# Attention scores seeded with their negated row maxima by ScalarE and VectorE, in place of a fourth matmul product

## The chip, the cores and the metric

The kernel runs on one core of a Trainium2 chip. The metric is the device time of one execution in microseconds; lower is better. The engines are TensorE (PE in the profile), VectorE (DVE), ScalarE (ACT), GpSimd (POOL) and the sync engine (SP), which only issues transfers.

## The reference

A self-attention block on x of shape (4, 512, 48, 48), that is 4 batches of 512 channels by T = 2304 tokens. With 32 groups of channels and 8 heads of 64 channels:

```python
xn = group_norm(x) * gn_w + gn_b
q, k, v = split(qkv_w @ xn + qkv_b)              # per head, 64 channels each
weight = softmax(q.T @ k / 8, axis=-1)           # 2304 x 2304 per head, fp32
a = v @ weight.T
out = xn + proj_w @ a + proj_b
```

The softmax takes each query's maximum over all keys off its scores before the exponential. Scores are made from a high and a low part of q and k (fp32r values), so that three products give nearly fp32 precision.

## The kernel before

The work runs as 4 batches, each of 4 head pairs. A pair's queries are cut into CH = 6 blocks of N = 384, and its keys into KT = 18 tiles of 128. A *step* is one key tile against one query block for both heads of the pair; a block has 18 steps, a batch 432. Two steps make a *slot* (GS = 2), so a block has 9 slots, numbered 0 to 8 here. Every engine has its own program with its instructions in a fixed order, and semaphores join them. In slot i, with steps 2i and 2i+1, the engines do the following.

- **TensorE**: one *max unit* (`max_unit`, L498: 128 queries against 384 keys, high parts only, for both heads, into `aux_banks`), then `make_scores` for step 2i and step 2i+1 (L532, four products each: k_hi q_hi, k_lo q_hi, k_hi q_lo, and one_rows max_row, each for two heads), then a second max unit, then a part of the projections (*prep*) of a later q, k or v chunk into `pool_bank` (L476, L488), then `make_pv` for the steps of the slot before (L550). In slot 2 of a block, `finish` (L519) sums the denominators. The max units run AHEAD = 24 steps ahead of the scores, since a query's maximum must be known before its scores are finished.
- **ScalarE**: `exponentials` for both steps (L743, from the scores bank to one of 8 `probs` buffers), then what a finished prep needs (`high_part` L692 or `v_group` L696), and once per block the copies of `oacc` (L728) and of the sums (L708).
- **VectorE**: for each max unit a reduction over 384 keys (`unit_max`, L842), which frees `aux_banks` for the next unit, since there is only one such buffer; in slots 3, 4 and 5 of a block one piece of a reciprocal per step (`take_recip`, L917), the last followed by the product `o_norm` (L923, both inputs in SBUF); the low part of a finished q or k chunk (`low_part`, L835); and at step 11 of a block, in slot 5, `negate_max` (L848), which reduces the 6 partial maxima of 3 x 128 queries and both heads. Pair 3 of the first three batches also has the statistics of the next batch (L864) and its coefficients (L882 to L908).
- **GpSimd**: adds each step's probabilities into `denom` (L1057), 17 additions of 128x768 per block. An exponential waits for the addition of 8 steps before.
- **SP**: weights, x, the results and `put_max_row` (L350).

The negated maxima lie in columns, one query per partition, and the scores need them in a row. `max_rows` (L504) turns them over with one TensorE product against `ident`, ScalarE copies them (L703), and two small transfers put them into `max_row`. The fourth product then adds that row to each score.

The last pair of the last batch has no max units. After the four pairs of a batch comes its output projection (L631), and at the start of a batch ScalarE waits until the previous batch's output is stored. In the pairs 0 to 2, three preps are spread over each block in quarters by `SPREAD`; pair 3 runs them whole in written slots.

Of the kernel before, what the change touches and what calls it, by code (L numbers as in the profile page):

```python
# [5 lines left out]
def attention_block_program(nc, x, gn_w, gn_b, wqkv_t, bqk, bv, wproj_t, bproj, att, out):  # L6
# [47 lines left out]
    SPREAD = (((0, 0, 2), (1, 2, 4)), ((3, 0, 1), (4, 1, 3), (5, 3, 4)), ((7, 0, 2), (8, 2, 4)))  # L54
# [10 lines left out]

    def maxrow_slot(j):
        last_unit = QT * CH * (j + 1) - 1
        return (last_unit - AHEAD) // GS + 1

    def batch_plan(more_batches):  # L70
# [7 lines left out]
        for p in range(PAIRS):  # L78
# [17 lines left out]
            for j in range(1, CH):  # L96
                whole(before, s0 + maxrow_slot(j), ("maxrow", p, j))
            if p < PAIRS - 1 or more_batches:
                whole(before, s0 + SLOTS + maxrow_slot(0), ("maxrow", p + 1, 0))
# [26 lines left out]
    def first_order():  # L126
# [7 lines left out]
        order.append(("maxrow", 0, 0))  # L134
# [26 lines left out]

    with ExitStack() as ctx:
# [10 lines left out]
        max_row = sb("max_row", [128, T], fp32r)  # L173
        one_rows = sb("one_rows", [128, 128], fp32r)
# [15 lines left out]
        ident = sb("ident", [128, 128])  # L190
# [3 lines left out]
        neg_max = sb("neg_max", [128, D])  # L194
        row_parts = sb("row_parts", [2 * QT, 128], fp32r)
# [70 lines left out]
        aux_done = sem("aux_done")  # L266
        neg_ready = sem("neg_ready")
        max_row_in = sem("max_row_in")
# [61 lines left out]
        def _(sp):  # L330
# [15 lines left out]
            def put_max_row(j, u):  # L346
                wait_free(sp, u)
                for e in range(2):
                    dst = max_row[e * D:e * D + 1, chunk(j)].bitcast(fp32).rearrange("o (t q) -> o t q", q=128)
                    sp.dma_start(dst, row_parts[e * QT:(e + 1) * QT, :].bitcast(fp32)).then_inc(max_row_in, 16)  # L350
# [7 lines left out]
            def stream(b, last):  # L358
                before, _ = PLANS[last]
                nb = b + 1  # L360
                for s in range(BSTEPS):
# [10 lines left out]
                    if s in NORM_STEPS and not last and NORM_STEPS[s] + XPARTS < XITEMS:  # L372
                        n = NORM_STEPS[s]
                        sp.wait_ge(xn_ready, XITEMS * (b + 1) + n + 1)
                        load_x(nb, XITEMS + n + XPARTS)
                    if s in PUT_AT:
                        put_block(b, PUT_AT[s])
                    if s % GS < GS - 1:
                        continue
                    for key in completed(before[s // GS]):  # L380
                        if key[0] == "maxrow":
                            put_max_row(key[2], use(b, last, key))
                        elif key == ("q", p, CH - 1) and not (last and p == PAIRS - 1):
# [55 lines left out]
            put_max_row(0, FIRST_USES["maxrow", 0, 0])  # L439
# [13 lines left out]
            sp.wait_ge(max_row_in, 32 * BLOCKS * B)  # L453
# [5 lines left out]
        def _(pe):  # L459
# [63 lines left out]
            def score_part(s, b, product):  # L523
                p, j, kt = s // STEPS, s % STEPS // KT, s % KT
                if product == 0 and s >= 2:
                    pe.wait_ge(probs_ready, PROBS_PRIMED + BSTEPS * b + s - 1)
                elif product == 3 and kt == 0:
                    pe.wait_ge(max_row_in, 32 * (BLOCKS * b + p * CH + j + 1))
                ks, qs = ((k_hi[p % 2], q_hi), (k_lo[p % 2], q_hi), (k_hi[p % 2], q_lo), (one_rows, max_row))[product]
                kcols = slice(kt * 128, (kt + 1) * 128) if product < 3 else slice(0, 128)  # L530
                for e in range(2):
                    last = mm(scores[:, s % 2, e, 0:N], ks[head(e), kcols], qs[head(e), chunk(j)],  # L532
                              start=(product == 0), stop=(product == 3))
                if product == 3:
                    last.then_inc(scores_full, 1)

            def make_scores(s, b):
                for product in range(4):
                    score_part(s, b, product)
# [26 lines left out]
            def behind(key, since, until, b, last):  # L566
# [18 lines left out]
                elif kind == "maxrow":  # L585
                    max_rows(CH * pairs + i + 1, u)
# [51 lines left out]
            pe.wait_ge(consts_made, 8)  # L638
            units = 0
            for key in FIRST:  # L640
# [23 lines left out]
                elif kind == "maxrow":  # L664
                    max_rows(1, u)
# [7 lines left out]
            for k in range(FIRST_BANKS):  # L673
                pe.wait_ge(bank_free[k], first_count(k))

# [10 lines left out]
        def _(act):  # L686
# [11 lines left out]

            def max_rows(u, rows_sent):
                wait_full(act, u)  # L700
                if rows_sent is not None:
                    act.wait_ge(max_row_in, rows_sent)
                a(row_parts[:, :], bank(u)[0:2 * QT, 0:128], ACT.Copy).then_inc(bank_free[u[0]], 1)  # L703
# [41 lines left out]

            def behind(key, b, last):
# [8 lines left out]
                elif kind == "maxrow":  # L755
                    max_rows(u, 32 * (CH * (PAIRS * b + p) + i))
# [5 lines left out]
            def stream(b, last):  # L762
                before, after = PLANS[last]
                for i in range(PAIRS * SLOTS):
# [31 lines left out]
            for s in (o_saved, proj_saved):  # L796
# [322 lines left out]
```

## Time and profile before

| | before |
|---|---|
| median of 3 runs | 4161.06 us (4151.73 to 4162.0) |
| profiled execution, its own time | 4164.19 us |
| its span | 4162.4 us |
| granted TensorE clock in it | 0.991 |
| PE / DVE / ACT / POOL busy | 97% / 55% / 41% / 72% |

A row of the timeline gives the start, the duration, the engine, the line, the operation, what it writes and reads, how many instructions are merged, and in brackets the idle time before it and what ended that. The duration of a merged group is that of the whole group. Matmuls overlap, so the pitch between the starts of two groups tells what one costs, and not its duration.

### The profile page before, as it was taken

How to read it: one execution, taken by the hardware profiler on the slowest of the kernel's cores; microseconds unless marked ns; L12 is line 12 of the kernel's file. 1: busy time of each engine (PE TensorE's matmuls, PEld its weight loads, DVE VectorE, ACT ScalarE, POOL GpSimd, SP SyncE). 2: the span in 40 equal slices, each digit the busy share in tenths (PEclk: the TensorE clock that was granted, in tenths of full speed). 3: DMA queues.
4: the chain of work that ended last, by engine and by line, in shares of the span. 5: the costliest groups of instructions: out<-in, count | busy, mean ns of one | idle time of the engine just before them, and what ended most of it. 6: DMA issues, size and time to landing. Idle time of an engine off the chain costs nothing.

```text
span 4162.4 us, 86380 instructions
## 1 busy us (share of the span) xinstructions
PE 4034.5 (97%) x33648; PEld 2660.7 (64%) x33648; DVE 2285.1 (55%) x2982; ACT 1723.8 (41%) x2487; POOL 3009.8 (72%) x1641
## 2 busy tenths in 40 slices
PE   6999999999899999999989999999999999999997
PEld 4666666656766666665676656666567666666666
DVE  4555555574455555556545555556654555555553
ACT  2443444454344444445334444444543444444443
POOL 0777778777378787777737877877773877777793
PEclk9999999999999999999999999999999999999999
DMA  2000000020400000012040000001103000000004
GB/s 69 8 8 12 8 10 12 29 80 10 142 8 10 10 10 10 10 41 67 12 140 10 10 8 10 12 8 57 53 25 124 12 8 10 10 10 7 7 7 141
DMA packets 116464, 128.16 MB, mean 31 GB/s; under 512 B 56080, under 2 KB 105808, under 8 KB 115536
## 3 DMA queue, kind: packets, MB, share of 16 engines
q1 hardware_dynamic: 116048, 122.49, 9.4%
q8 instruction: 275, 4.51, 0.4%
q14 instruction: 141, 1.16, 0.1%
HBM read 84.43 MB, written 37.75 MB: 29 GB/s over the span
## 4 chain that ended last, share of the span: by engine, by line
PE 85%; DVE 4%; issue 3%; DMA 3%; POOL 3%; SPq 0%; ACT 0%; DVEq 0%; POOLq 0%; ACTq 0%
PE scores L532 26%; PE oacc L550 25%; PE pool_bank L476 12%; PE aux_banks L498 11%; PE pool_bank L488 6%; POOL denom L1057 3%; DVE maxima L842 2%; PE scores L631 2%; PE pool_bank L519 1%; DMA att_in<-att 1%; DMA out<-probs 1%; DVE recip L917 1%; PE pool_bank L504 1%; PE scores L476 1%; DVE probs L991 0%
## 5 line engine op out<-in xcount | busy, mean ns | idle before, releaser
L1057 POOL TENSOR_TENSOR denom<-denom,probs 128x768 f32<-128x768 f32 x1536 | 2834.5, 1845 | 652.6 <-ACT probs L743 552.8
L842 DVE TENSOR_REDUCE maxima<-aux_banks 128x2 f32<-128x768 f32 x1728 | 1656.9, 959 | 1432.4 <-PE aux_banks L498 1430.1
L743 ACT ACTIVATE probs<-scores 128x768 f32<-128x768 f32 x1728 | 1308.2, 809 | 1602.0 <-PE scores L532 1155.0
L550 PE MATMUL oacc<-probs,vals 128*64 128x384 f32 x6912 | 1303.0, 492 | 0.0
L550 PEld LDWEIGHTS oacc<-probs,vals 128*64 128x64 f32 x6912 | 505.3, 137 | 475.4 <-issue 438.3
L498 PE MATMUL aux_banks<-k_hi,q_hi 64*128 64x384 f32 x3456 | 692.3, 394 | 54.8 <-DVE maxima L842 47.0
L498 PEld LDWEIGHTS aux_banks<-k_hi,q_hi 64*128 64x128 f32 x3456 | 329.5, 184 | 599.1 <-issue 409.2
L532 PE MATMUL scores<-q_hi,k_lo 64*128 64x384 f32 x3456 | 593.0, 335 | 0.0
L532 PE MATMUL scores<-q_hi,k_hi 64*128 64x384 f32 x3456 | 589.7, 335 | 2.7 <-ACT probs L743 2.7
L532 PE MATMUL scores<-q_lo,k_hi 64*128 64x384 f32 x3456 | 591.4, 334 | 0.0
L532 PE MATMUL scores<-max_row,one_rows 64*128 64x384 f32 x3456 | 590.7, 334 | 0.0
L1054 POOL TENSOR_TENSOR denom<-probs 128x768 f32<-128x768 f32 x96 | 174.3, 1816 | 438.4 <-ACT probs L743 438.4
L917 DVE RECIPROCAL recip<-sums 128x64 f32<-128x64 f32 x556 | 309.2, 557 | 47.4 <-ACT sums L708 47.4
L532 PEld LDWEIGHTS scores<-max_row,one_rows 64*128 64x128 f32 x3456 | 335.1, 185 | 0.0
L532 PEld LDWEIGHTS scores<-q_hi,k_hi 64*128 64x128 f32 x3456 | 327.5, 186 | 10.8 <-ACT probs L743 9.4
L532 PEld LDWEIGHTS scores<-q_lo,k_hi 64*128 64x128 f32 x3456 | 331.5, 185 | 0.0
L532 PEld LDWEIGHTS scores<-q_hi,k_lo 64*128 64x128 f32 x3456 | 328.3, 185 | 0.0
L476 PE MATMUL pool_bank<-xn,wq 128*64 128x384 f32 x1504 | 284.8, 499 | 0.0
L488 PE MATMUL pool_bank<-wv,xn 128*64 128x128 f32 x4416 | 282.6, 277 | 0.0
L476 PE MATMUL pool_bank<-xn,wk 128*64 128x384 f32 x1456 | 276.1, 499 | 0.0
L488 PEld LDWEIGHTS pool_bank<-wv,xn 128*64 128x64 f32 x4416 | 237.2, 137 | 46.9 <-issue 46.9
L476 PEld LDWEIGHTS pool_bank<-xn,wq 128*64 128x64 f32 x1504 | 91.1, 136 | 114.2 <-issue 114.2
(94 smaller groups left out, 1590.9 us busy)
## 6 DMA issues: line engine op xcount, KB each, us to landing
xtile<-x SPq DMA_DIRECT2D x72, 384.0 KB, 3.2
att<-o_norm SPq DMA_DIRECT2D x96, 192.0 KB, 1.9
att_in<-att SPq DMA_DIRECT2D x24, 768.0 KB, 6.4
probs<-x SPq DMA_DIRECT2D x24, 768.0 KB, 4.6
out<-probs SPq DMA_DIRECT2D x24, 768.0 KB, 5.5
xn<-x SPq DMA_DIRECT2D x4, 1152.0 KB, 8.6
wk<-wqkv_t SPq DMA_DIRECT2D x32, 128.0 KB, 2.4
wq<-wqkv_t SPq DMA_DIRECT2D x32, 128.0 KB, 2.4
```

The source lines that it names most:

```text
L476: last = mm(to[head(e), 0:N], w[:, k, head(e)], xn[:, k, chunk(c)], start=(k == 0), stop=(k == CT - 1))
L488: last = mm(to[head(half), i * 128:(i + 1) * 128], xn[:, k, t0:t0 + D], wv[:, k, :], start=(k == 0), stop=(k == CT - 1))
L498: last = mm(aux_banks[:, e, 0:N], q_hi[head(e), qt * 128:(qt + 1) * 128], k_hi[p % 2][head(e), chunk(kc)], start=True, stop=True)
L504: filled(mm(bank_for(u)[0:D, 0:128], neg_max[:, :], ident[:, :], start=True, stop=True), u)
L532: last = mm(scores[:, s % 2, e, 0:N], ks[head(e), kcols], qs[head(e), chunk(j)], start=(product == 0), stop=(product == 3))
L550: ins = mm(oacc[head(e), 0:N], vals[p % 2][:, kt, head(e)], prob(s)[:, e * N:(e + 1) * N], start=(kt == 0), stop=(kt == KT - 1))
L631: last = mm(scores[:, n // 2 % 2, n % 2, 0:N], w[:, k, ot * 128:(ot + 1) * 128], a[:, k, :], start=(not low and w is wproj_hi and k == 0), ...
L743: a(prob(s).rearrange("p (h n) -> p h n", n=N), scores[:, s % 2, :, 0:N], ACT.Exp, scale=SCALE).then_inc(probs_ready, 1)
L842: v.tensor_reduce(maxima[:, :, qt, kc], aux_banks[:, :, 0:N], AX.X, ALU.max).then_inc(aux_done, 1)
L917: last = v.reciprocal(recip[:, cs], sums[:, cs])
L1054: gp.tensor_tensor(acc, prob(s - 1), prob(s), ALU.add).then_inc(added, 1)
L1057: gp.tensor_tensor(acc, acc, prob(s), ALU.add).then_inc(added, 1)
```

## The change

The fourth product is gone, with `max_rows`, `ident`, `one_rows` and `max_row`. Before the first of three products of a step, another engine writes the negated maxima into the step's PSUM slot as a 128x768 copy from an SBUF tile `seeds`, and the products add to it (`start=False`). ScalarE writes the even steps and VectorE the odd ones. Each engine does so in slot i for a step of slot i+1, after its exponentials (ScalarE), or after its two `unit_max` and what else the steps have (VectorE), and before its work on finished preps. The copy for step s+2 waits for the exponential of step s, which is the slot's last reader, and the score products wait for the copy. The negated maxima are turned over by a VectorE 32x32 block transpose, sent to a tensor in DRAM by four transfers, and read back into all 128 partitions by one. `SPREAD` is changed: slot 5 takes half of a prep where it took a quarter, slot 4 a quarter where it took half, and the third prep starts in slot 6. `open_banks` runs four products once, before the first batch.

```diff
-    SPREAD = (((0, 0, 2), (1, 2, 4)), ((3, 0, 1), (4, 1, 3), (5, 3, 4)), ((7, 0, 2), (8, 2, 4)))
+    SPREAD = (((0, 0, 2), (1, 2, 4)), ((3, 0, 1), (4, 1, 2), (5, 2, 4)), ((6, 0, 1), (7, 1, 2), (8, 2, 4)))
...
+            def send_max(n, blk):
+                par = blk % 2
+                sp.wait_ge(neg_ready, n + 1)
+                for i in range(4):
+                    sp.dma_start(neg_rows[:, 32 * i:32 * (i + 1)], neg_cols[32 * i:32 * i + 2 * QT, :])\
+                      .then_inc(neg_out, 16)
+                sp.wait_ge(neg_out, 64 * (n + 1))
+                if not isinstance(n, int) or n >= 2:
+                    for slot in range(2):
+                        sp.wait_ge(seeded[slot], PRIMED + KT // 2 * (n - 1))
+                sp.dma_start(seeds[par][:, :], neg_rows.rearrange("r q -> (r q)").partition_broadcast(128))\
+                  .then_inc(seeds_in[par], 16)
...
-            def max_rows(n, u):
-                pe.wait_ge(neg_ready, n)
-                filled(mm(bank_for(u)[0:D, 0:128], neg_max[:, :], ident[:, :], start=True, stop=True), u)
...
+            def make_scores(s, b):
                 p, j, kt = s // STEPS, s % STEPS // KT, s % KT
+                keys = slice(kt * 128, (kt + 1) * 128)
+                pe.wait_ge(seeded[s % 2], PRIMED + BSTEPS // 2 * b + s // 2 + 1)
+                for n, (ks, qs) in enumerate(((k_hi[p % 2], q_hi), (k_lo[p % 2], q_hi), (k_hi[p % 2], q_lo))):
+                    for e in range(2):
+                        last = mm(scores[:, s % 2, e, 0:N], ks[head(e), keys], qs[head(e), chunk(j)],
+                                  start=False, stop=(n == 2), skip_group_check=True)
+                last.then_inc(scores_full, 1)
...
+            def seed(s, b):                                   # ScalarE
+                blk = s // KT
+                if s % KT < 2:
+                    act.wait_ge(seeds_in[blk % 2], 16 * (BLOCKS // 2 * b + blk // 2 + 1))
+                if s < 2:
+                    act.wait_ge(banks_opened, 1)
+                    act.wait_ge(proj_saved, PRIMED + PJ * b)
+                else:
+                    act.wait_ge(probs_ready, PROBS_PRIMED + BSTEPS * b + s - 1)
+                a(scores[:, s % 2, :, 0:N], seeds[blk % 2].rearrange("p (e n) -> p e n", n=N), ACT.Copy)\
+                    .then_inc(seeded[s % 2], 1)
...
                     for s in range(GS * i, GS * i + GS):
                         exponentials(s, b)
+                    if GS * i + 2 < BSTEPS:
+                        seed(GS * i + 2, b)
                     for key in completed(before[i]):
                         behind(key, b, last)
...
+                v.tensor_reduce(neg_max[:, 0:2 * QT].rearrange("p (e t) -> p e t", t=QT),
+                                maxima[:, :, QT * j:QT * (j + 1), :], AX.X, ALU.max, negate=True)\
+                    .then_inc(negated, 1)
...
+                v.transpose(neg_cols[:, :], neg_max[:, :]).then_inc(neg_ready, 1)
...
                     for s in range(GS * i, GS * i + GS):      # VectorE
                         unit_of_step(s, b, last)
                         for blk, piece in PIECES_AT.get(s, ()):
                             take_recip(b, blk, use(b, last, ("finish", blk // CH, blk % CH)), (piece,), PIECES)
                         if s in STATS_STEPS and not last:
                             take_stats(STATS_STEPS[s], b + 1)
+                    if GS * i + 3 < BSTEPS:
+                        seed(GS * i + 3, b)                   # tensor_copy, else as ScalarE's
                     for key in completed(before[i]):
                         behind(key, b, last)
```

## Rows read from the trace of the kernel before

**Rows 1.** The page: busy time by engine, and the chain by line.
```profile
PE 4034.5 (97%) x33648; PEld 2660.7 (64%) x33648; DVE 2285.1 (55%) x2982; ACT 1723.8 (41%) x2487; POOL 3009.8 (72%) x1641
...
PE scores L532 26%; PE oacc L550 25%; PE pool_bank L476 12%; PE aux_banks L498 11%; PE pool_bank L488 6%; POOL denom L1057 3%; DVE maxima L842 2%; PE scores L631 2%; PE pool_bank L519 1%; DMA att_in<-att 1%; DMA out<-probs 1%; DVE recip L917 1%; PE pool_bank L504 1%; PE scores L476 1%; DVE probs L991 0%
```

**Rows 2.** Groups by line: busy us, mean ns, idle before.
```profile
L923 DVE TENSOR_TENSOR o_norm<-o_raw,recip 128x384 f32<-128x384 f32 x96 | 64.3, 670 | 17.6 <-DVE recip L917 16.8
...
L848 DVE TENSOR_REDUCE neg_max<-maxima 128x6 f32<-128x36 f32 x96 | 18.3, 191 | 9.7
```

**Rows 3.** Timeline of one slot with half a prep, all engines.
```profile
1606.20 0.44 PE L498 MATMUL aux_banks<-k_hi,q_hi 64*128 64x384 f32 x2
...
1606.48 0.33 PE L532 MATMUL scores<-q_hi,k_hi 64*128 64x384 f32 x2
...
1606.69 0.96 DVE L842 TENSOR_REDUCE maxima<-aux_banks 128x2 f32<-128x768 f32 x1 [2.14 <-PE aux_banks L498]
...
1607.01 0.34 PE L532 MATMUL scores<-max_row,one_rows 64*128 64x384 f32 x2
...
1607.38 1.52 ACT L743 ACTIVATE probs<-scores 128x768 f32<-128x768 f32 x2 [0.50 <-PE scores L532]
...
1607.87 0.36 PE L498 MATMUL aux_banks<-k_hi,q_hi 64*128 64x384 f32 x2
...
1608.16 1.51 PE L476 MATMUL pool_bank<-xn,wq 128*64 128x384 f32 x8
...
1608.36 3.72 POOL L1057 TENSOR_TENSOR denom<-denom,probs 128x768 f32<-128x768 f32 x2 [2.17 <-ACT probs L743]
...
1609.50 1.46 PE L550 MATMUL oacc<-probs,vals 128*64 128x384 f32 x8
...
1610.89 0.45 PE L498 MATMUL aux_banks<-k_hi,q_hi 64*128 64x384 f32 x2
```

**Rows 4.** Timeline of the first preps: a max unit that waits for the one before.
```profile
79.53 0.44 PE L498 MATMUL aux_banks<-k_hi,q_hi 64*128 64x384 f32 x2 [1.14 <-DVE maxima L842]
79.91 2.84 PE L488 MATMUL pool_bank<-wv,xn 128*64 128x128 f32 x48
...
83.16 0.96 DVE L842 TENSOR_REDUCE maxima<-aux_banks 128x2 f32<-128x768 f32 x1 [2.19 <-PE aux_banks L498]
84.17 0.44 PE L498 MATMUL aux_banks<-k_hi,q_hi 64*128 64x384 f32 x2 [1.06 <-DVE maxima L842]
```

**Rows 5.** Timeline of a slot 5 that began at 359.37, and the next.
```profile
361.53 3.72 POOL L1057 TENSOR_TENSOR denom<-denom,probs 128x768 f32<-128x768 f32 x2 [0.95 <-ACT probs L743]
...
363.75 1.92 DVE L923 TENSOR_TENSOR o_norm<-o_raw,recip 128x384 f32<-128x384 f32 x1 [0.57 <-DVE recip L917]
...
367.12 0.44 PE L498 MATMUL aux_banks<-k_hi,q_hi 64*128 64x384 f32 x2 [1.85 <-DVE maxima L842]
```

**Rows 6.** The chain of waits, in order of time, in the slot after that.
```profile
367.56 0.25 PE pool_bank L504
367.81 2.61 PE oacc L550 x8
```

**Rows 7.** Timeline of the end of a usual slot 5, and the next.
```profile
1627.69 0.56 DVE L923 TENSOR_TENSOR o_norm<-o_raw,recip 128x384 f32<-128x384 f32 x1 [0.22 <-DVE recip L917]
1627.71 0.45 PE L498 MATMUL aux_banks<-k_hi,q_hi 64*128 64x384 f32 x2
...
1629.70 0.44 PE L498 MATMUL aux_banks<-k_hi,q_hi 64*128 64x384 f32 x2
```

**Rows 8.** Windows: busy us (and instructions) of PE, PEld, DVE, ACT, POOL, then the granted clock.
```profile
367.80:370.60 2.80, 2.80 (x12) 1.25 (x9) 0.76 (x1) 0.27 (x1) 1.48 (x1) 0.51 0.01 1
...
861.68:900.68 39.00, 34.24 (x264) 21.42 (x264) 30.05 (x46) 19.46 (x26) 31.04 (x18) 0.96 0.20 57
...
3932.24:3963.91 31.67, 31.67 (x260) 20.46 (x262) 20.68 (x26) 14.76 (x21) 29.52 (x17) 1.00 0.02 8
```

**Rows 9.** Timeline: SP issues the two transfers of a maxima row.
```profile
1630.91 1.38 SPq L350 DMA_DIRECT2D max_row<-row_parts  x2
```

More of the change, by code:

```diff
@@ L95, in batch_plan @@
                     whole(before, s0 + s, key)
[L96 to L99, printed above, removed]
             for j in range(CH):
@@ L160, in unit_at, with ends_block, block_of @@
         return u // STEPS, u % STEPS // CH, u % CH
+    neg_rows = nc.dram_tensor("neg_rows", (2 * QT, 128), fp32, kind="Internal").ap()
+    def ends_block(unit):
+        _, qt, kc = unit
+        return kc == CH - 1 and qt % QT == QT - 1
+    def block_of(unit):
+        p, qt, _ = unit
+        return p * CH + qt // QT
     with ExitStack() as ctx:
@@ L172, in attention_block_program @@
         k_lo = [sb(f"k_lo{i}", [128, T], fp32r) for i in range(2)]
-        max_row = sb("max_row", [128, T], fp32r)
-        one_rows = sb("one_rows", [128, 128], fp32r)
+        seeds = [sb(f"seeds{i}", [128, 2 * N]) for i in range(2)]
         xn = sb("xn", [128, CT, T])
@@ L266, in attention_block_program @@
         aux_done = sem("aux_done")
+        negated = sem("negated")
         neg_ready = sem("neg_ready")
-        max_row_in = sem("max_row_in")
+        neg_out = sem("neg_out")
+        seeds_in = [sem(f"seeds_in{i}") for i in range(2)]
+        banks_opened = sem("banks_opened")
+        seeded = [sem(f"seeded{i}") for i in range(2)]
         scores_full = sem("scores_full")
@@ L375, in stream @@
                         load_x(nb, XITEMS + n + XPARTS)
+                    unit = unit_at(s, last)
+                    if unit is not None and ends_block(unit):
+                        blk = block_of(unit)
+                        send_max(BLOCKS * b + blk, blk)
                     if s in PUT_AT:
@@ L380, in stream @@
                     for key in completed(before[s // GS]):
-                        if key[0] == "maxrow":
-                            put_max_row(key[2], use(b, last, key))
-                        elif key == ("q", p, CH - 1) and not (last and p == PAIRS - 1):
+                        if key == ("q", p, CH - 1) and not (last and p == PAIRS - 1):
                             wait_full(sp, use(b, last, key))
@@ L452, in _ @@
             sp.wait_ge(att_out, PRIMED + 16 * BLOCKS * B)
-            sp.wait_ge(max_row_in, 32 * BLOCKS * B)
+            for par in range(2):
+                sp.wait_ge(seeds_in[par], 16 * BLOCKS // 2 * B)
             for signal in (wq_in, wk_in, wv_in):
@@ L521, in finish, with open_banks @@
                 filled(last, u)
-            def score_part(s, b, product):
+            def make_scores(s, b):
                 p, j, kt = s // STEPS, s % STEPS // KT, s % KT
[L525 to L539, printed above, removed]
+                keys = slice(kt * 128, (kt + 1) * 128)
[5 more added lines that the diff above has]
+                last.then_inc(scores_full, 1)
+            def open_banks():
+                for slot in range(2):
+                    for e in range(2):
+                        last = mm(scores[:, slot, e, 0:N], k_hi[0][head(e), 0:128], q_hi[head(e), chunk(0)],
+                                  start=True, stop=True)
+                last.then_inc(banks_opened, 1)
             def make_pv(s, b, last):
@@ L795, in _ @@
             act.sem_inc(probs_ready, PROBS_PRIMED)
-            for s in (o_saved, proj_saved):
+            for s in (o_saved, proj_saved, seeded[0]):
                 act.sem_inc(s, PRIMED)
@@ L812, in _ @@
                         a(wproj_hi[:, :, :], wproj_full, ACT.Copy).then_inc(wproj_hi_ready, 1)
-                elif kind == "maxrow":
-                    max_rows(u, None)
             def batch(b, last):
@@ L939, in unit_of_step @@
                 unit_max(AHEAD + BSTEPS * b + s, qt, kc, rows)
-                if kc == CH - 1 and qt % QT == QT - 1:
-                    key = ("maxrow", p, qt // QT)
-                    u = use(b, last, key)
-                    negate_max(qt // QT, units_done(b, s), rows_before(b, last, key))
-            def rows_before(b, last, key):
-                uses = [k for k in USES[last] if k[0] == "maxrow"]
-                i = uses.index(key)
-                return use(b, last, uses[i - 1]) if i else None
+                if ends_block(unit):
+                    negate_max(qt // QT, units_done(b, s), rows)
             def behind(key, b, last):
@@ L1018, in _ @@
                     units += 1
-                elif kind == "maxrow":
-                    negate_max(0, QT * CH, None)
+                    if units == QT * CH:
+                        negate_max(0, units, None)
             dve.wait_ge(wproj_hi_ready, 1)
@@ L1059, in _ @@
             pool.sem_inc(added, PRIMED)
-            gp.memset(ident[:, :], 0.0).then_inc(masks_filled, 1)
             gp.memset(groups[:, :], 1.0 / GROUP).then_inc(masks_filled, 1)
-            pool.wait_ge(masks_filled, 2)
-            gp.affine_select(out=ident[:, :], in_=ident[:, :], compare_op=ALU.not_equal, fill=1.0,
-                             base=0, pattern=[[-1, 128]], channel_multiplier=1).then_inc(consts_made, 2)
+            pool.wait_ge(masks_filled, 1)
             gv = groups[:, :].rearrange("p (g c) -> p g c", c=GROUP)
```

59 lines of the change are left out of this document (25 added, 34 removed).

## The prediction

> **What bounds the kernel now.** I read the page first, then the groups by line, then the timeline of single slots, since an average over 864 slots does not show which wait ends last. TensorE is busy for 97% of the span, and L532, L550, L476 and L498 carry most of the chain [rows 1]. It looks bound by TensorE, and the fourth product looks like pure gain. The slot shows how thin that is. From its start, taken as 0, TensorE issues the first max unit at 0, the scores at 0.28, the second unit at 1.67, the prep at 1.96, the pv products at 3.30, and the next slot starts at 4.69 [rows 3]. The fourth product of the first step starts 0.53 us after its first, three pitches, so one product for two heads costs 0.175 us. Half a prep costs 1.34 us, so a slot without prep takes 4.69 - 1.34 = 3.35.
>
> VectorE has its own loop in this. Its reduction of the first unit starts at 0.49 and ends at 1.45 [rows 3]. As `aux_banks` is a single buffer, the second unit cannot start sooner. Where a unit does wait, it starts 0.05 us after the reduction's end (83.16 + 0.96 = 84.12, then 84.17), and what follows it starts 0.38 us after it (79.53 to 79.91) [rows 4], against 0.29 where it did not wait (1607.87 to 1608.16) [rows 3].
>
> **Removed: the fourth product.** Two per slot, 0.35 us, over 864 slots 302 us. What counts is when the work behind the second unit starts, now 1.96. Without the products TensorE reaches the unit at 1.67 - 0.35 = 1.32, but the reduction ends at 1.45; the unit starts at 1.50 and the next work at 1.50 + 0.38 = 1.88. So a slot gains 0.08 us, and the rest becomes a wait for VectorE: a plain slot takes 3.27. `max_rows` also goes, 0.25 us per block (L504 in [rows 6]). A block gains 9 x 0.08 + 0.25 = 0.97.
>
> **Added: the copies.** No row shows a 128x768 copy into PSUM. ScalarE's nearest are the exponentials of the same width, 1.52 us for two [rows 3], so 0.76; as ends I take 0.76 and VectorE's 0.96. The first exponential starts 0.37 us after the last product (1607.01 to 1607.38), so now at 1.00; the second ends at 2.5, the copy at 3.3 to 3.5. In a plain slot the scores that it releases are due at 3.27 + 0.28 = 3.55. It is covered, by 0.1 us at worst.
>
> VectorE's nearest row is the reduction of 768 elements, 0.96 us [rows 3]. The ends are half of that, 0.48 (two elements in one pass), and 0.96 plus the wait for one GpSimd addition of 1.86 [rows 3], 2.8 us. I take 0.96, the nearest in width and engine. Back to back, I estimate that VectorE's instructions overlap by 0.09. The second reduction now runs from 1.98 to 2.94, the copy to 3.81; the next slot's reduction wants to start at 3.27 + 0.49 = 3.76. So even the plain slot has no VectorE slack left.
>
> **Slot 5 is where it breaks.** VectorE has there: reductions to 2.94, `negate_max` to 3.26, the new transpose to about 3.45 (nearest row L848, 191 ns [rows 2]; ends 0.1 and 0.4 with its waits), the last reciprocal piece, `o_norm`, the copy, in 4 of 6 blocks `low_part` (0.6), and then the reduction that the next max unit waits for. GpSimd's additions start at 2.16 in a slot, and the first ends at 4.02 [rows 3]. The usual `o_norm` starts at 1627.69, which is 4.0 in its slot (a quarter of a prep, 4.02 long, before 1627.71): just ahead of the second addition, and takes 0.56 [rows 7]. In the slot that began at 359.37 it came too late: the additions ran from 361.53 to 365.25, `o_norm` ended at 365.67, and the max unit waited until 367.12 [rows 5]. With the change GpSimd's first addition starts at 2.0 (exponential at 1.00, not 1.18) and ends at 3.86, and `o_norm`, delayed by the transpose, asks at 4.2. I expect it to miss and to wait until after 5.72. Then the copy runs from 6.06 to 7.02, `low_part` to 7.55, the reduction to 8.42; the unit starts at 8.47. It is due at 4.61 + 1.50 = 6.11, so 2.36 late, without `low_part` 1.80, mean 2.2. Today the same unit starts 1.99 after its slot and not 1.67 [rows 7], 0.3 late with `low_part`, mean 0.2. Net per block of pairs 0 to 2: -0.97 + 2.2 - 0.2 = +1.0 us; 72 blocks, +72.
>
> After the 1.85 us of idle the granted clock was 0.51 for 2.8 us [rows 8], the 1.2 GHz level, and eight pv instructions took 2.61 us [rows 6] and not 1.3, so 1.3 us more. The new wait is in two pieces, for the copy (about 1.7) and for the unit (0.9). I take this cost for one block in four, 72/4 x 1.3 = +23 (ends 0 and +94). The one block per batch that pays it all today falls out: -4 x 3.3 = -13.
>
> The Trainium skill (SBUF — State Buffer, Who interferes with whom) says that a VectorE copy contends with GpSimd only in a two-port mode, and (VectorE: DVE Perf Modes, Why PSUM operands drop a tier) that a PSUM operand rules that mode out; by the pages the copy keeps 1x rate and waits for no addition. No row here shows such a copy.
>
> **Pair 3.** In blocks with statistics VectorE is busy for 30.05 of 39.00 us [rows 8], and waits already; nine copies of 0.87 net are 7.8 us, of which I let half to two thirds through: +3 and +5 for the first two blocks, +1 each for the next three; three batches, +33 (ends 0 and 60). The last batch's pair 3 takes 31.67 us per block [rows 8] with 17 additions of 1.86, 31.6: GpSimd bounds it before and after, 0. **Batch starts**: ScalarE is held there by the stores; scores and a prep run ahead of it, and will wait for its first copy, by estimate 0.8 and the products and unit behind, 2.3 us, 4 times: +9. **Transfers**: five issues at 0.69 (1.38 for two [rows 9]) are 3.5 us, and two flights; from slot 5 at 3.5 to the first copies of the next block are some 11.5 us. Unless the flights take over 8 us together, nothing is seen.
>
> **Sum**: 4164.2 + 72 + 23 - 13 + 33 + 9 = 4288 in the profiled execution's own time, which is 3 us above the median: 4285.
>
> **The rivals.** *The forecast*, 0.54. *`o_norm` gets in*, 0.22: the phase turns out well. Then the unit in slot 6 is 1.0 or 0.45 late, mean 0.84, a block nets -0.97 + 0.84 - 0.2 = -0.33: 4161 - 24 - 13 + 33 + 9 = 4166; with a copy of 0.48 us another 0.45 per block off, 4134. For it speaks that all but a few do today (mean 670 ns [rows 2]); against it, that today's margin is a few hundredths. *TensorE stays the bound*, 0.08, the other side: the second unit does start at 1.32. The place is the second max unit, the price 0.27 us per slot, 233 us, and it decides from a reduction that ends before 1.32. That is 4285 - 233 = 4052, and 4161 - 302 - 24 = 3835 if slot 5 is not late either. Every unit that waits today speaks against it [rows 4, 5]. *Transfers late*, 0.08: each microsecond beyond the budget costs 96 us, 4381 for one; nothing here shows a write to DRAM read back at once. *The copy meets GpSimd*, 0.08: it waits for the additions, which fill 3.7 us of a slot, ends at 4.4 and not 3.8, and slot 5 loses 1 us more: 4285 + 72 = 4357.
>
> **How the numbers follow.** A measurement here tells 0.3% from no change: 4148.6 to 4173.5. Faster: *TensorE stays the bound*, and half of *`o_norm` gets in*: 0.19. Within: the other half and the forecast's low edge, 0.14. Slower: 0.67. The range leaves out the TensorE case and the worst of the late transfers: 4120 to 4370. The likeliest case alone runs from 4225 to 4350.
>
> **What would show it.** A plain slot of 3.27 and not 3.0 us; the second max unit waiting for L842's reduction in most slots; TensorE busy well under 97%; VectorE near 73% (2285 + 864 x 0.96 of 4285); its copies near 0.96; `o_norm` with a median near 1.9; the unit in slot 6 late by about 2 us. Copies of 0.5, a median of 0.56 for `o_norm`, or scores that wait for the transfers would make it wrong.

## The result and the profile after

The changed kernel takes 4279.9 us (median of 4 runs, 4262.94 to 4284.98) against 4161.07 us (4151.73 to 4162.0): ratio 1.0281, 95% interval 1.0267 to 1.0296, 119 us slower. The profiled execution took 4283.88 us, span 4282.2 us, granted clock 0.973. The forecast was 4288 for the profiled execution and 4285 for the median.

The page after: busy time by engine, three of the costliest groups, and the issue of the new read-back (packets, KB each, median us to landing). It answers to [rows 1] and [rows 2].

```profile
PE 4002.0 (93%) x30004; PEld 2337.7 (55%) x30004; DVE 3124.3 (73%) x3940; ACT 2328.3 (54%) x3255; POOL 2994.3 (70%) x1639
...
L882 DVE COPY scores<-seeds 128x768 f32<-128x768 f32 x864 | 819.4, 948 | 23.2 <-ACT probs L747 22.6
L760 ACT ACTIVATE scores<-seeds 128x768 f32<-128x768 f32 x864 | 708.5, 820 | 4.3 <-DMA out<-probs 4.3
L957 DVE TENSOR_TENSOR o_norm<-o_raw,recip 128x384 f32<-128x384 f32 x96 | 147.6, 1538 | 17.0 <-DVE recip L951 16.1
...
seeds<-neg_rows SPq DMA_DIRECT2D x96, 384.0 KB, 3.5
```

TensorE has lost only 32.5 us of busy time (4034.5 to 4002.0), where the products left out had taken about 302. Busy time is not the cost of the work: the durations of products overlap, less so beside a wait (a product of a max unit now counts 444 ns in the mean, before 394), and more of the span ran at the lower clock (0.973 for 0.991). VectorE has gained 839, and `o_norm` has gone from 670 ns to 1538 in the mean. No maxima row was late: the read-back lands after 3.5 us.

The waits, one line from before and then the lines after, by what was waited for (us in total, times, longest):

```profile
PEld aux_banks L498 <- DVE maxima L842: 185.4, 267, 4.8
...
PEld aux_banks L514 <- DVE maxima L858: 399.6, 945, 6.1
PEld scores L542 <- DVE scores L882: 161.2, 116, 4.4
PE scores L542 <- DVE scores L882: 122.7, 90, 4.0
```

Before, the max unit's weight load (PEld) waited for the reduction 267 times, now 945 times. A handshake in nearly every slot is what the forecast put there. The timeline after, one slot with half a prep up to the work behind its second unit; it answers to [rows 3]:

```profile
1624.40 0.44 PE L514 MATMUL aux_banks<-k_hi,q_hi 64*128 64x384 f32 x2
...
1629.02 0.45 PE L514 MATMUL aux_banks<-k_hi,q_hi 64*128 64x384 f32 x2
...
1629.51 0.96 DVE L858 TENSOR_REDUCE maxima<-aux_banks 128x2 f32<-128x768 f32 x1 [1.30 <-PE aux_banks L514]
...
1630.52 0.44 PE L514 MATMUL aux_banks<-k_hi,q_hi 64*128 64x384 f32 x2
1630.89 1.53 PE L504 MATMUL pool_bank<-wv,xn 128*64 128x128 f32 x24
```

From 1624.40 to 1629.02 is 4.62 us (forecast 3.27 + 1.34 = 4.61; before 4.69). The second unit starts 1.50 after the first, 0.05 after the reduction's end (1629.51 + 0.96 = 1630.47), and the next work 0.37 behind it (forecast 1.50, 0.05 and 0.38). Two products less per slot have bought 0.07 us.

The timeline after, a slot 5 (it starts at 1691.78) and the next, TensorE, VectorE and GpSimd; it answers to [rows 7], and in what happens to [rows 5]:

```profile
1691.78 0.44 PE L514 MATMUL aux_banks<-k_hi,q_hi 64*128 64x384 f32 x2
...
1693.76 3.73 POOL L1084 TENSOR_TENSOR denom<-denom,probs 128x768 f32<-128x768 f32 x2 [0.23 <-ACT probs L747]
...
1695.95 1.95 DVE L957 TENSOR_TENSOR o_norm<-o_raw,recip 128x384 f32<-128x384 f32 x1 [0.22 <-DVE recip L951]
1696.39 0.45 PE L514 MATMUL aux_banks<-k_hi,q_hi 64*128 64x384 f32 x2
...
1697.83 0.95 DVE L882 COPY scores<-seeds 128x768 f32<-128x768 f32 x1
...
1699.21 0.94 DVE L858 TENSOR_REDUCE maxima<-aux_banks 128x2 f32<-128x768 f32 x1
1700.21 0.44 PE L514 MATMUL aux_banks<-k_hi,q_hi 64*128 64x384 f32 x2 [0.58 <-DVE maxima L858]
```

`o_norm` starts 4.17 after the slot's start (forecast 4.2), when the second of two additions is running, and lasts until 1697.90, 0.41 after that addition's end at 1697.49. The copy starts at 6.05 (forecast 6.06). The max unit in slot 6 is due at 1696.39 + 1.50 = 1697.89 and starts at 1700.21, 2.32 late (forecast 2.36 with `low_part`).

`o_norm` in the middle of batch 1 and of the last batch (duration min/median/max in ns), and the end of a slot 5 of the last batch, that began at 3560.83:

```profile
L957 DVE TENSOR_TENSOR o_norm<-o_raw,recip x21: 567/1948/2079, 1245.8 to 2084.5; 128x384 f32<-128x384 f32 x21
...
L957 DVE TENSOR_TENSOR o_norm<-o_raw,recip x21: 557/559/2147, 3230.6 to 4070.0; 128x384 f32<-128x384 f32 x21
...
3564.16 0.51 DVE L951 RECIPROCAL recip<-sums 128x64 f32<-128x64 f32 x1
3564.70 0.56 DVE L957 TENSOR_TENSOR o_norm<-o_raw,recip 128x384 f32<-128x384 f32 x1
...
3564.78 2.18 POOL L1084 TENSOR_TENSOR denom<-denom,probs 128x768 f32<-128x768 f32 x1
```

In the last batch it gets in, most of the time. It asks at 3564.70 - 3560.83 = 3.87 and the second addition starts at 3.95: here VectorE has no 0.22 us of idle between the reciprocal and `o_norm`, as it has in the other batches, and the addition is the one that is held up (2.18 and not 1.86). In one run it meets the lock at 4.17 and gets in at 3.87, 0.3 us apart. Of the 18 products `o_norm` of pairs 0 to 2, all miss in each of the first three batches and one misses in the last. The last batch is written out and the others come from one body; that this makes the 0.22 us is argued, no run changed it.

The windows after, from the first copy of `oacc` of a batch to the 18th (17 blocks of pairs 0 to 2): us, then busy of PE, PEld, DVE, ACT, POOL, granted clock (the last two numbers are of the DMA engines). The last row is pair 3 of batch 0, from the 18th to the 24th copy.

```profile
145.98:857.58 711.60, 679.13 (x5142) 382.06 (x5144) 531.39 (x648) 386.99 (x545) 527.60 (x289) 0.96 0.07 21
1225.27:1922.18 696.91, 664.17 (x5142) 376.17 (x5144) 531.36 (x648) 387.00 (x545) 527.55 (x289) 0.99 0.07 21
...
3351.14:4012.09 660.95, 651.64 (x5142) 372.03 (x5144) 508.47 (x646) 385.33 (x545) 533.59 (x289) 1.00 0.07 19
857.58:1116.13 258.55, 236.34 (x1772) 132.22 (x1770) 198.66 (x267) 148.92 (x204) 183.34 (x101) 0.95 0.19 56
```

The same stretches before:

```profile
144.79:820.54 675.75, 672.59 (x5788) 434.30 (x5788) 374.49 (x478) 280.60 (x409) 532.92 (x289) 1.00 0.04 12
1168.78:1844.61 675.83, 672.66 (x5788) 434.38 (x5788) 374.46 (x478) 280.56 (x410) 532.92 (x289) 1.00 0.04 12
...
3222.11:3892.71 670.60, 670.38 (x5788) 433.40 (x5790) 373.85 (x476) 279.39 (x410) 529.55 (x289) 1.00 0.03 9
820.54:1062.65 242.11, 234.41 (x1996) 150.39 (x1994) 148.89 (x209) 111.67 (x158) 184.00 (x100) 0.99 0.18 50
```

The 119.8 us of span come from three places: the blocks of pairs 0 to 2, +35.9, +21.1, +21.1 (batch 2 is as batch 1) and -9.7, in all +68.4; pair 3, +16.4 in batch 0, and 15.2, 12.8 and 4.4 in the others by the same windows, +48.9; the rest +2.5, of which +6.5 lie ahead of the first copies of the four batches (a block each in it) and -4.0 after the last.

Single blocks show what those means are made of. Three of the changed kernel (two of batch 0, one of the last batch), then two of the kernel before:

```profile
649.70:691.90 42.20, 40.11 (x270) 20.72 (x270) 31.79 (x39) 22.81 (x32) 31.02 (x17) 0.96 0.08 21
691.90:732.42 40.52, 38.40 (x270) 20.31 (x270) 31.79 (x39) 22.82 (x32) 31.04 (x17) 1.00 0.05 16
3428.82:3467.67 38.85, 38.22 (x286) 21.02 (x288) 30.40 (x39) 22.71 (x32) 31.40 (x17) 1.00 0.08 23
...
1208.37:1247.93 39.56, 39.43 (x308) 23.90 (x308) 22.45 (x29) 16.61 (x24) 31.37 (x17) 1.00 0.02 6
1366.12:1409.04 42.92, 41.07 (x308) 24.72 (x308) 23.80 (x29) 16.61 (x25) 30.95 (x17) 0.96 0.02 6
```

A block whose `o_norm` misses takes 40.52, one in which the clock falls as well 42.20, and one in which `o_norm` gets in 38.85, for 39.56 before. The last row is the one late block that each of the first three batches already had before; the last batch had none.

### The profile page after: what moved, and what is told of

It is laid out like the page before. It is cut to its first block, busy times and chain, and to the rows that moved or that the text cites. A ratio compares the mean times of both kernels' runs of the same rounds, so it can differ in the third digit from the quotient of the medians.

```text
span 4282.2 us, 82304 instructions
## 1 busy us (share of the span) xinstructions
PE 4002.0 (93%) x30004; PEld 2337.7 (55%) x30004; DVE 3124.3 (73%) x3940; ACT 2328.3 (54%) x3255; POOL 2994.3 (70%) x1639
## 3 DMA queue, kind: packets, MB, share of 16 engines
q14 instruction: 170, 1.39, 0.1%
## 4 chain that ended last, share of the span: by engine, by line
PE 78%; DVE 11%; issue 6%; DMA 2%; POOL 2%; ACT 1%; SPq 0%; DVEq 0%; POOLq 0%; ACTq 0%
PE oacc L563 23%; PE scores L542 18%; PE aux_banks L514 15%; PE pool_bank L492 11%; PE pool_bank L504 6%; DVE maxima L858 5%; PE scores L642 3%; DVE scores L882 2%; POOL denom L1084 2%; PE pool_bank L531 1%; DVE recip L951 1%; DMA att_in<-att 1%; DMA out<-probs 1%; DVE stats L898 1%; PE scores L492 0%
## 5 line engine op out<-in xcount | busy, mean ns | idle before, releaser
L514 PE MATMUL aux_banks<-k_hi,q_hi 64*128 64x384 f32 x3456 | 773.0, 444 | 75.7 <-DVE maxima L858 62.4
L882 DVE COPY scores<-seeds 128x768 f32<-128x768 f32 x864 | 819.4, 948 | 23.2 <-ACT probs L747 22.6
L563 PEld LDWEIGHTS oacc<-probs,vals 128*64 128x64 f32 x6912 | 479.7, 140 | 526.5 <-issue 500.6
L542 PE MATMUL scores<-q_hi,k_hi 64*128 64x384 f32 x3456 | 604.7, 346 | 149.2 <-DVE scores L882 122.7
L760 ACT ACTIVATE scores<-seeds 128x768 f32<-128x768 f32 x864 | 708.5, 820 | 4.3 <-DMA out<-probs 4.3
L492 PE MATMUL pool_bank<-xn,wq 128*64 128x384 f32 x1504 | 299.5, 514 | 0.0
L504 PE MATMUL pool_bank<-wv,xn 128*64 128x128 f32 x4416 | 294.9, 282 | 0.0
L957 DVE TENSOR_TENSOR o_norm<-o_raw,recip 128x384 f32<-128x384 f32 x96 | 147.6, 1538 | 17.0 <-DVE recip L951 16.1
```

The source lines that it names most:

```text
L492: last = mm(to[head(e), 0:N], w[:, k, head(e)], xn[:, k, chunk(c)], start=(k == 0), stop=(k == CT - 1))
L504: last = mm(to[head(half), i * 128:(i + 1) * 128], xn[:, k, t0:t0 + D], wv[:, k, :], start=(k == 0), stop=(k == CT - 1))
L514: last = mm(aux_banks[:, e, 0:N], q_hi[head(e), qt * 128:(qt + 1) * 128], k_hi[p % 2][head(e), chunk(kc)], start=True, stop=True)
L542: last = mm(scores[:, s % 2, e, 0:N], ks[head(e), keys], qs[head(e), chunk(j)], start=False, stop=(n == 2), skip_group_check=True)
L563: ins = mm(oacc[head(e), 0:N], vals[p % 2][:, kt, head(e)], prob(s)[:, e * N:(e + 1) * N], start=(kt == 0), stop=(kt == KT - 1))
L760: a(scores[:, s % 2, :, 0:N], seeds[blk % 2].rearrange("p (e n) -> p e n", n=N), ACT.Copy)\
```

## The experiments

All times are medians with the ratio to the kernel before, timed together on the same chip. The kernel before had 4158.11 us beside the first four kernels, 4164.68 beside the next four and 4157.52 beside the last four.

**First set: is it the handshake, and is it `o_norm`?** `no4` is the kernel before without its fourth product; its scores lack the maxima, and the row is still made, sent and waited for. The two "onein" kernels put a one-input copy of `o_raw` in the place of `o_norm`, so the division is left out. `after_act_seeds` is the changed kernel with both copies on ScalarE; it waits for the second exponential of the slot before the first copy.

```diff
 # no4
-                for product in range(4):
+                for product in range(3):
-                elif product == 3 and kt == 0:     # the wait for the row
+                elif product == 2 and kt == 0:
 # no4_onein, after_onein
-v.tensor_tensor(o_norm[:, :], o_raw[:, :], recip[:, :], ALU.mult).then_inc(o_normed, 1)
+v.tensor_copy(o_norm[:, :], o_raw[:, :]).then_inc(o_normed, 1)
 # after_act_seeds: ScalarE's slot; VectorE's seed() is gone
+                    act.wait_ge(probs_ready, PROBS_PRIMED + BSTEPS * b + GS * i + 2)
                     seed(GS * i + 2, b)
+                    seed(GS * i + 3, b)
```

> The kernel before, with only the fourth product left out (so the maxima are not taken off the scores; the row is still made and waited for). My theory (the second max unit waits for the reduction, and o_norm for GpSimd): a slot gains 0.08 us and not 0.35, and GpSimd's additions move forward by 0.18 us in a slot, so o_norm is at the edge of missing its gap: 4105 us if it still gets in, 4250 if it misses and waits in most blocks. Rival (TensorE is the bound, a product is worth its pitch): 4161 - 302 = 3860.

> As no4, and o_norm becomes a plain copy of o_raw, with one SBUF input and not two (so the division by the sums is left out too). My theory: no wait for GpSimd is left, only the wait of the second max unit: 4161 - 96 x 0.75 = about 4090. Rival (TensorE is the bound): 3860, the same as no4. If no4 is also near this one, o_norm's wait played no part in it.

> The changed kernel with o_norm as a plain copy of o_raw (the division by the sums is left out), everything else in place. My theory: slot 5 loses the wait of about 1.4 us, the unit in slot 6 is 1.0 or 0.45 us late and not 2.3 or 1.8, and the falls of the clock go with it: 4280 - 72 x 1.35 - 25 - 20 = about 4140. Rival (the VectorE copies' own time is the loss, not the wait for GpSimd): 4260 to 4280.

> The changed kernel with ScalarE writing the odd steps too, right behind the even ones; VectorE writes none. My theory: o_norm still asks at 4.2 us and waits, but the reduction in slot 6 comes 0.87 us sooner, the unit is 1.5 or 0.9 late: 4280 - 65 - 15 - 25 = about 4175. Rival A (VectorE's total work of copies is the whole loss): near 4000. Rival B (ScalarE's chain of two exponentials and two copies now ends last): over 4280.

Measured: `no4` 4217.29 us, 1.0142 (1.0125 to 1.0159); `no4_onein` 4199.08, 1.0098 (1.0081 to 1.0115); `after_onein` 4238.57, 1.0185 (1.0165 to 1.0206); `after_act_seeds` 4180.28, 1.0052 (1.0035 to 1.0069). `o_norm` in `no4`, by tile, and the total of the waits of its max units:

```profile
L923 DVE TENSOR_TENSOR o_norm<-o_raw,recip x96: 557/2169/2198, 167.8 to 4156.9; 128x384 f32<-128x384 f32 x96
...
PEld aux_banks L498 <- DVE maxima L842: 536.7, 1014, 5.2
```

Taking 302 us of products away, with nothing added, makes the kernel 59 us slower. That alone rules out that TensorE stays the bound, and it is nothing about the copies: the second unit waits, the phase of the slot moves, and `o_norm` falls into the additions (median 2169 ns). Expected were 4105 us if it still got in and 4250 if it missed; it missed in all blocks of pairs 0 to 2 of the first three batches and in none of the last.

Both "onein" kernels missed their expectations by about 100 us, because their premise failed. `no4_onein`, by tile and in one slot's timeline:

```profile
L923 DVE COPY o_norm<-o_raw x96: 359/1982/2018, 167.8 to 4138.5; 128x384 f32<-128x384 f32 x96
...
1655.71 3.73 POOL L1057 TENSOR_TENSOR denom<-denom,probs 128x768 f32<-128x768 f32 x2 [0.88 <-ACT probs L743]
...
1657.66 1.98 DVE L923 COPY o_norm<-o_raw 128x384 f32<-128x384 f32 x1 [0.22 <-DVE recip L917]
```

A copy between SBUF tiles takes 359 ns when free and 1982 in the median: it waits for GpSimd's addition as the product of two inputs did. The copy into PSUM does not, with 948 ns in the mean over 864. The Trainium skill (SBUF — State Buffer, Who interferes with whom) names both kinds that contend with GpSimd, a VectorE instruction with two SBUF inputs and a copy in a two-port mode; these rows agree, with 2169 and 1982 ns, and the experiment should have been laid out by it. In `after_onein` the median is 1747 ns. The copies moved to ScalarE take VectorE's 0.96 us out of the way: 4180.28 us where about 4175 was expected, 100 gained against the changed kernel, though `o_norm` still misses (median 2007 ns). So this run does not tell the lock's part from the copy's.

**Second set: `o_norm` away from the lock.** GpSimd itself does the product, with the same three waits, behind the addition of step 11 of the next block. This was built on the kernel before, on `no4`, on the changed kernel and on `after_act_seeds`.

```diff
 # VectorE, after the last reciprocal piece: three waits and the product go
-                    v.tensor_tensor(o_norm[:, :], o_raw[:, :], recip[:, :], ALU.mult).then_inc(o_normed, 1)
 # GpSimd
                 for s in range(BSTEPS):
                     add(s, b)
+                    if s in PUT_AT:
+                        normalized(b, PUT_AT[s])     # same waits, gp.tensor_tensor
```

> The changed kernel with o_norm made by GpSimd, in its own queue behind the addition of step 11, so that VectorE has no instruction left that waits out a GpSimd addition in pairs 0 to 2. My theory: the unit in slot 6 is 0.3 us late and not 2.3, the falls of the clock in these pairs go: 4280 - 144 - 23 - 10 = about 4100, blocks of 38.5. Rival (VectorE's volume of work in slot 5 is the loss; after_onein took only 41 us off): 4230.

> The kernel before with o_norm on GpSimd, the control. There o_norm gets in already in all but a few blocks, so only VectorE's 0.56 us and the four late blocks are to be gained, and GpSimd has 0.96 us more per block where it is the bound: about 4135 by my theory. If it gains as much as after_pool_norm does, the move helps for another reason than the wait.

> The kernel before without the fourth product (the maxima are not taken off), and with o_norm on GpSimd: what the removal alone is worth once no lock is met. My theory (the second unit waits for the reduction): 0.08 us per slot less than before_pool_norm, about 4135 - 65 = 4070. Rival (TensorE bound, a product is worth its pitch): 4135 - 302 = 3833.

> The changed kernel with both copies on ScalarE and o_norm on GpSimd. My theory: nothing is late in slot 5 any more and only the handshake of the max units is left, as in no4_pool_norm: blocks of 38.3, about 4075. Rival (ScalarE ends last): over 4180, no better than after_act_seeds.

| kernel | with `o_norm` on VectorE | on GpSimd | ratio to before (95%) |
|---|---|---|---|
| before | 4164.68 | 4140.54 | 0.9945 (0.9929 to 0.9962) |
| changed | 4279.9 | 4108.97 | 0.9869 (0.9853 to 0.9886) |
| no4 (maxima not added) | 4217.29 | 4082.13 | 0.9806 (0.979 to 0.9822) |
| changed, ScalarE writes both | 4180.28 | 4099.22 | 0.9843 (0.9826 to 0.9859) |

The expectations were about 4100, 4135, 4070 and 4075 for `after_pool_norm`, `before_pool_norm`, `no4_pool_norm` and `after_act_pool`; the last came out 24 us above, the others 5 to 12. In the last three rows the two columns were timed apart, and the median of the kernel before differed by up to 7 us between the sets. In `after_pool_norm`, the group of `o_norm` and a slot 5 that starts at 1671.36:

```profile
L1086 POOL TENSOR_TENSOR o_norm<-o_raw,recip 128x384 f32<-128x384 f32 x96 | 101.8, 1061 | 20.2 <-DVE recip L951 20.2
...
1671.36 0.44 PE L514 MATMUL aux_banks<-k_hi,q_hi 64*128 64x384 f32 x2
...
1675.21 0.94 DVE L882 COPY scores<-seeds 128x768 f32<-128x768 f32 x1
...
1675.96 0.45 PE L514 MATMUL aux_banks<-k_hi,q_hi 64*128 64x384 f32 x2
```

The copy of slot 5 now starts at 3.85 and not at 6.05, and nothing else of the change is touched. Moving this one instruction, 96 of them, is worth 171 us in the changed kernel and 24 in the kernel before. With it out of the way in both, the change is 31.6 us faster (4140.54 to 4108.97) where it had been 119 slower.

The 171 us are more than the wait. The move also takes the product's own 0.56 us off VectorE, and the clock's falls go with it: 17 blocks of batch 1 take 653.27 us at 1.00 where they took 696.91 at 0.99.

```profile
1156.46:1809.73 653.27, 650.24 (x5142) 372.90 (x5144) 498.50 (x631) 385.21 (x545) 544.02 (x306) 1.00 0.08 22
```

Where the copies do not stand behind it on VectorE, the same move is worth less: 135 us in `no4` and 81 with both copies on ScalarE. What the meeting alone costs can be estimated from the last batch, where `o_norm` stays on VectorE and gets in: its 17 blocks are 9.7 us faster than before, -41 for all 72, in place of +72. By that the meeting, with the falls of the clock behind it, is 113 of the 119 us lost, so nearly all of it. The last batch differs from the others in being written out, so this is an estimate, and the experiment shows it only together with the product's own time.

The rows of `before` and `no4` give the value of the product itself: 4140.54 - 4082.13 = 58.4 us, 0.068 per slot, where the forecast had 0.08 for the same two products (69) and the price on TensorE is 0.35 (302). What the copies, the transposes and the transfers cost, less the 24 us of `max_rows`, is 4108.97 - 4082.13 = 26.8; ScalarE for VectorE brings 10 of it back.

**Third set: the handshake itself.** If the second unit waits for the reduction, putting half of the pv products ahead of it should hide the wait. The pv products are eight in a slot, four for each step. The order costs something too, since TensorE changes from pv products to a unit and back once more per slot, so the kernel before was run in that order as a control. `act_pool_order` is `after_act_pool` in the new order. `after_old_spread` is the changed kernel with the `SPREAD` of before, a quarter of a prep in slot 5.

```diff
 # before_order, after_order, act_pool_order
                     make_scores(second, b)
+                    if i:
+                        make_pv(first - 2, b, last)
                     unit_of_step(second, b, last)
                     for key, since, until in before[i]:
                         behind(key, since, until, b, last)
                     if i:
-                        make_pv(first - 2, b, last)
                         make_pv(first - 1, b, last)
 # after_old_spread
-    SPREAD = (((0, 0, 2), (1, 2, 4)), ((3, 0, 1), (4, 1, 2), (5, 2, 4)), ((6, 0, 1), (7, 1, 2), (8, 2, 4)))
+    SPREAD = (((0, 0, 2), (1, 2, 4)), ((3, 0, 1), (4, 1, 3), (5, 3, 4)), ((7, 0, 2), (8, 2, 4)))
```

> after_act_pool with TensorE's order changed: the pv products of one of the two steps run before the slot's second max unit and not after it, so that the unit comes when the reduction of the first is over. My theory: the 0.27 us per slot that the change gave to the wait come back, less about 0.1 us for one more change between kinds of products; plain slots stay bound by VectorE; blocks of 36.8 us, 4099 - 90 x 1.5 = about 3965. Rival (TensorE's own rate or GpSimd's additions, 31.6 us per block and 1 for o_norm, bound it already): 4080 to 4100.

> The kernel before with the same change of TensorE's order alone, as a control. There the second unit waits for no reduction, so nothing is to be gained, and the extra change between kinds of products costs about 0.1 us in 864 slots: about 4230. If it is faster than 4161, the order helps for another reason.

> The changed kernel with the change of TensorE's order alone. My theory: the wait of the second unit goes, but slots 3 to 6 hang on VectorE with its copies and on o_norm's wait, which the order does not touch; a small gain at best, 4200 to 4280. Rival (the wait of the second unit is the whole loss): 4280 - 233 = 4050.

> The changed kernel with the old SPREAD of the preps. Slot 5 is then 0.67 us shorter and slot 4 as much longer, so the unit in slot 6 is due sooner and late by 3.0 and not 2.3 us: about 4330. If it is 4280 or less, the new spread was worth nothing here.

Measured: `act_pool_order` 4152.52 us (10 runs), 0.9991 (0.9981 to 1.0001); `before_order` 4487.4, 1.0798 (1.078 to 1.0816); `after_order` 4364.87, 1.0499 (1.0481 to 1.0516); `after_old_spread` 4352.89, 1.0484 (1.0461 to 1.0506). The expectations were about 3965, 4230, 4200 to 4280, and 4330: all four came out slower, the third as a loss of 85 us where a small gain was expected. The timeline of `before_order`, TensorE, the end of one slot and the next:

```profile
1651.55 0.45 PE L498 MATMUL aux_banks<-k_hi,q_hi 64*128 64x384 f32 x2
1651.93 0.87 PE L550 MATMUL oacc<-probs,vals 128*64 128x384 f32 x4
...
1653.65 0.34 PE L532 MATMUL scores<-q_hi,k_hi 64*128 64x384 f32 x2
...
1655.16 0.87 PE L550 MATMUL oacc<-probs,vals 128*64 128x384 f32 x4
1655.95 0.45 PE L498 MATMUL aux_banks<-k_hi,q_hi 64*128 64x384 f32 x2
1656.33 0.88 PE L488 MATMUL pool_bank<-wv,xn 128*64 128x128 f32 x12
1657.04 0.81 PE L550 MATMUL oacc<-probs,vals 128*64 128x384 f32 x4
1657.78 0.45 PE L498 MATMUL aux_banks<-k_hi,q_hi 64*128 64x384 f32 x2
```

The control cost 330 us, 0.38 per slot, where I had estimated 0.1. Four pv products ahead of a unit take 0.79 (1655.16 to 1655.95) and the other four 0.74 (1657.04 to 1657.78), together 1.53, where eight in a row take 1.39 in [rows 3] (1609.50 to 1610.89); and the work behind a unit starts 0.38 after it in place of 0.29 (1651.55 to 1651.93). The third place is the change from scores to pv products: from the first score product to the work behind the last is 1.51 (1653.65 to 1655.16), where it is 1.39 when a max unit follows, in [rows 3] (1606.48 to 1607.87). The three, 0.14, 0.09 and 0.12, come to 0.35 of the 0.38.

Against this cost the order gave back part. On the changed kernel it came to +85.0 us and on `after_act_pool` to +53.3, where the control says +330; the differences, 245 and 277, are what less waiting returned, near the 0.27 x 864 = 233 at which the forecast priced the handshake. That the return is all handshake is not shown: in `after_order` `o_norm` also has a median of 926 ns, since the phase moved again, and the granted clock is 0.988 for 0.973. So `act_pool_order` missed its expectation by 188 us mainly for the price of the order, not for the handshake's. No order was found that has the one without the other.

The old `SPREAD` makes the changed kernel 73 us slower. `o_norm` has the same median (1939 ns), and the granted clock is lower, 0.963 for 0.973, which by the spans takes away up to 4350.6 x 0.037 - 4282.2 x 0.027 = 45 us more. So the new one is not what loses, and part of what it gives can be the clock. That it helps because TensorE has half a prep of work in slot 5 while VectorE is late is argued, no run took it apart.

## Why the prediction came out right

**The slot.** Plain slot 3.27: the slot with half a prep took 4.62 for a forecast of 4.61. The gain of 0.08 us and not of 0.35 stands in `no4_pool_norm` (0.068), without any copy. This was the step that decided the sign, and it came from two rows: when TensorE could start the second unit, and when the reduction that frees its only buffer ended.

**The copies.** VectorE's 948 ns (forecast 0.96) and ScalarE's 820 (0.76 to 0.96). The row of the same width on the same engine was the right price in both cases. The rival *the copy meets GpSimd* is out by the 948.

**Slot 5.** `o_norm` asked at 4.17, the copy began at 6.05 and the unit was 2.32 late, for 4.2, 6.06 and 2.36. The move to GpSimd (171 us) shows the place. A block that misses, with no fall of the clock, took 40.52 for 39.56 before, and over the 27 blocks of this kind in the first three batches the mean is 40.43 for 39.56, so +0.9 where the forecast had +1.0. Wrong was that all 72 blocks would do this: in 17 of the 18 of the last batch it got in, and its blocks were 0.57 us faster. The rival *`o_norm` gets in* has its own block at -0.33, and it lives in a quarter of the kernel. So this term is 54 x 0.9 - 18 x 0.57, about +38, and not +72.

**The clock.** Forecast +23, for one fall of 1.3 us in every fourth block, and -13 for the late blocks that fall out. The falls came in 24 of the 51 blocks of the first three batches, twice in four of them, and in none of the last. Against the same blocks without a fall they cost 24.0 us in batch 0 and 9.3 in each of batches 1 and 2, 1.5 a fall, which is about +45 for the 54 blocks. Batch 0, with a granted clock of 0.96, is 14.7 us longer than batch 1 with 0.99 and the same instructions; why the falls are more frequent there stays open. The late blocks were three and not four, 42.92 for 39.56: about -10. After a late unit the clock was at the lower of its two levels, 1.2 GHz, while eight pv products ran, and 2.4 again when the next did. The timeline after, TensorE, and the window of that stretch:

```profile
675.89 2.73 PE L563 MATMUL oacc<-probs,vals 128*64 128x384 f32 x8
...
676.00:677.40 1.40, 1.40 (x8) 0.60 (x6) 0.70 (x1) 0.00 (x0) 0.69 (x1) 0.50 0.00 0
```

Blocks of pairs 0 to 2 with all of this: forecast 72 + 23 - 13 = 82, measured 68.4 for 68 of the 72, 72 for all at the same mean. Of what it is made, 38 + 45 - 10 and not 72 + 23 - 13, the forecast had the mechanisms right and the sizes wrong: that it was off by only 10 is luck.

**Pair 3 and the batch starts.** These two terms were mis-sized, against each other. Pair 3 cost 48.9 and not 33. The split was wrong too: 16.4, 15.2 and 12.8 in the first three batches, put at 11 each, and 4.4 in the last, which had been put at 0 because GpSimd bounds it. With 72 for all blocks, -1.5 is left for the rest of the kernel, where the batch starts were put at +9. How much of pair 3's is VectorE and how much the clock (0.95 for 0.99 in batch 0) was not tried apart. The sum, 4288, is 4 us off the profiled time, closer than its terms deserve, and that too is luck: measured less forecast is -10 for the blocks, +16 for pair 3 and -10 for the rest.

**Transfers.** Five issues were put at 0.69 each; four took 1.3 us together, 0.33 each. They were hidden at either price, as was said.

**The rivals.** *TensorE stays the bound* would have made `no4` 302 us faster, and it was 59 slower. *Transfers late* has nothing in the waits.

## What to carry over

Before crediting the removal of work from the busiest engine, find what in that stretch frees its next buffer and when: here 0.35 us of products stood in front of a reduction that ended 0.13 later than they would have, and 0.07 came back. Then carry the phase on through every instruction that takes part in a lock with another engine, since one such instruction per block was worth 171 us, and the whole change without it 32. Where it can go to the engine that holds the lock, that is worth trying first: the change with `o_norm` on GpSimd takes 4108.97 us, with both copies on ScalarE too 4099.22, both faster than the kernel before. Last, price the clock that falls after a late unit as a term of its own: here it was about as large as the wait.

## What the runs showed of the hardware

A 128x768 fp32 copy from SBUF to PSUM takes 948 ns on VectorE and 820 on ScalarE, and waits for no GpSimd addition (933 to 962 ns on VectorE over all 864, beside additions that took 70% of the span). A 128x384 fp32 copy within SBUF takes 359 ns on VectorE, but waits for a running addition (median 1982). The same product of two inputs takes 557 ns free on VectorE and 1061 on GpSimd. The blocked instruction ends 0.41 us after the addition does.

One more change per slot between pv products and max units, with the number of products the same, cost 0.38 us, more than two whole products at 0.35. That was the largest surprise, and 0.35 of it could be followed in the timeline: 0.14 for eight pv products in two fours, 0.12 at the change from scores to pv products and 0.09 behind the unit.
